# Moving table work, one transpose and two halves of a product in a hand-ordered four-engine pipeline (state-space convolution and routed low-rank FFN in fp32)

## The reference, cut to what matters

```python
# cond: a long convolution for each of 64 heads h, 64 states n
dtA = A * dt[:, None]                                   # A = -exp(log_A_real) + i A_imag
Cs  = Cc * (exp(dtA) - 1.0) / A
K   = 2.0 * einsum('hn,hnl->hl', Cs, exp(dtA * l)).real  # l = 0..1023
y   = irfft(rfft(u_m) * rfft(K)) + u_m * D               # u_m: u cut at each row's length
y   = y * mask
# ffn: 64 experts of rank 16, the top 16 of them for each token
scores = y @ Wr.T
gates  = softmax(top16(scores))                          # G: 0 for the other experts
h      = einsum('nd,krd->nkr', y, A)
out    = x + 2.0 * einsum('nkr,kdr->nd', h * G, B)
```

## Time and profile before

| | |
|---|---|
| median of 3 executions | 911.78 us |
| profiled execution, its own time | 912.11 us |
| its span, first to last instruction | 910.3 us |
| TensorE busy | 888.9 us (98%), 4536 matmuls |
| VectorE busy | 738.4 us (81%) |
| ScalarE busy | 380.7 us (42%) |
| 16 DMA engines | 40% of the span, 110 GB/s |
| mean granted TensorE clock | 0.998 |

### The profile page before, as it was taken

How to read it: one execution, slowest core, us unless ns; L and a number is a source line. 1 busy time by engine, 2 the same in 40 slices (tenths; PEclk the granted TensorE clock), 3 DMA queues, 4 the chain that set the end, 5 groups by cost and what they waited for, 6 DMA issues and landing times.

```text
span 910.3 us, 15546 instructions
## 1 busy us (share of the span) xinstructions
PE 888.9 (98%) x4536; PEld 791.5 (87%) x4536; DVE 738.4 (81%) x2473; ACT 380.7 (42%) x655; POOL 2.0 (0%) x12
## 2 busy tenths in 40 slices
PE   5999989999999999999999999999999999999998
PEld 4577978988999988899998899998889999889997
DVE  8899798888888888898888888888889888888722
ACT  4663344445334444434444533354443444442100
POOL 0000000000000000000000000000000000000000
PEclk9999999999999999999999999999999999999999
DMA  6631314443434443334443343444333444434331
GB/s 220 247 58 46 76 21 119 133 109 106 118 105 104 119 132 105 101 107 109 109 133 109 104 119 101 106 122 131 104 103 106 109 109 133 109 104 118 80 92 47
DMA packets 67123, 99.85 MB, mean 110 GB/s; under 512 B 22944, under 2 KB 49184, under 8 KB 67104
## 3 DMA queue, kind: packets, MB, share of 16 engines
q1 hardware_dynamic: 66400, 99.16, 39.8%
q10 hardware_dynamic: 704, 0.46, 0.2%
HBM read 60.52 MB, written 34.87 MB: 105 GB/s over the span
## 4 chain that ended last, share of the span: by engine, by line
PE 92%; DVE 4%; DMA 2%; ACT 1%; issue 1%; ACTq 0%; SPq 0%; DVEq 0%
PE out_ps L1239 25%; PE h_ps L1239 18%; PE out_ps L1243 12%; PE h_ps L1243 9%; PE turn_ps L1239 8%; PE turn_ps L1243 4%; PE conv_ps L1195 1%; PE conv_ps L1196 1%; PE conv_ps L1197 1%; PE h_ps L1248 1%; PE conv_ps L1178 1%; PE conv_ps L1179 1%; DMA b_in<-in_b_t 1%; PE conv_ps L1180 1%; PE conv_ps L1205 1%; PE conv_ps L1206 1%
## 5 line engine op out<-in xcount | busy, mean ns | idle before, releaser
L1239 PE MATMUL out_ps<-b_lo,g_hi 128*128 128x512 f32 x496 | 195.5, 394 | 0.0
L1239 PE MATMUL out_ps<-b_hi,g_hi 128*128 128x512 f32 x496 | 195.0, 393 | 0.0
L1239 PE MATMUL h_ps<-a_hi,y_hi 128*128 128x384 f32 x480 | 161.4, 336 | 0.0
L1239 PE MATMUL h_ps<-a_lo,y_hi 128*128 128x384 f32 x480 | 161.3, 336 | 0.0
L1243 PE MATMUL out_ps<-b_hi,g_lo 128*128 128x512 f32 x496 | 123.0, 390 | 0.0
L1243 PEld LDWEIGHTS out_ps<-b_hi,g_lo 128*128 128x128 f32 x496 | 93.1, 188 | 20.4
L1239 PEld LDWEIGHTS out_ps<-b_lo,g_hi 128*128 128x128 f32 x496 | 93.2, 188 | 19.6
L1239 PEld LDWEIGHTS out_ps<-b_hi,g_hi 128*128 128x128 f32 x496 | 93.2, 188 | 18.8
L715 DVE SCALAR_TENSOR_TENSOR z<-swapped,step_other,part 128x64 f32<-128x64 f32 x384 | 92.3, 281 | 12.0
L708 DVE SCALAR_TENSOR_TENSOR part<-z,step_own,conv_ps 128x64 f32<-128x64 f32 x384 | 90.3, 277 | 8.5
L1243 PE MATMUL h_ps<-a_hi,y_lo 128*128 128x384 f32 x480 | 93.1, 336 | 0.0
(11 more groups left out here) (216 smaller groups left out, 1496.6 us busy)
## 6 DMA issues: line engine op xcount, KB each, us to landing
xt_in<-in_xt SPq DMA_DIRECT2D x32, 512.0 KB, 3.3
x_in<-in_x SPq DMA_DIRECT2D x62, 256.0 KB, 3.6
out<-x_in SPq DMA_DIRECT2D x62, 256.0 KB, 3.1
moved<-square_sb SPq DMA_DIRECT2D x28, 512.0 KB, 2.6
square_sb<-moved SPq DMA_DIRECT2D x112, 128.0 KB, 2.9
b_in<-in_b_t SPq DMA_DIRECT2D x8, 512.0 KB, 6.0
a_in<-in_a_t SPq DMA_DIRECT2D x8, 512.0 KB, 7.1
t_lo<-k_sb SPq DMA_DIRECT2D x62, 64.0 KB, 4.1
```

What stands on the lines that cost most here:

```text
L1239: pe.matmul(o, hi[:, c, :], moving[:, c, columns], start=first and c == order[0] and moving is w_hi, stop=False)
```

## The change

Five edits, all in the order of instructions or in a wait; no arithmetic is added or removed.

1. **First step, ScalarE.** The split of the last `b` piece, MIDST[5], moves from ahead of `whole_in(1)` and `exps(0)` to behind them.
2. **Third step.** `arguments(4)` moves ahead of the last three chunks of `states(3)` on VectorE, `sines(4)` and `decays(4)` ahead of `high_z(3)` on ScalarE, `make_powers(4)` ahead of the two `low_gated(2)`, `out_factors(4)` between them; `high_in(4)`, `low_in(4)` and `arguments(5)` come earlier. On TensorE `turn_in(4)` moves ahead of `down(2, 0)`.
3. **step(3), VectorE.** `make_powers(5)` moves from behind the gate parts to a place ahead of the last three chunks of `states(4)`.
4. **step(3), TensorE.** `down(2, 1)` moves ahead of `kernel_row(5)` (it stood behind it).
5. **Last tile.** In `last_down` the single wait for both `add_rows(30)` becomes one for each bank of `out_ps`.

In the code of `step`, t is 3 where `second` is true. The iteration variable of the loop and the code of all later iterations are the same.

```diff
--- before.py
+++ after.py
@@ -469,7 +469,7 @@
             sines(1)
             decays(1)
             theta(2)
-            for i in MIDST[2:]:
+            for i in MIDST[2:5]:
                 split_weights(i)
 
             def exps(t):
@@ -501,6 +501,8 @@
             def first_step():
                 whole_in(1, in_ps_1)
                 exps(0)
+                for i in MIDST[5:]:
+                    split_weights(i)
                 copy_k(1, k_ps_1)
                 for i in LATE[:2]:
                     split_weights(i)
@@ -536,17 +538,17 @@
             def third_step():
                 exps(2)
                 high_near(3)
+                sines(4)
+                decays(4)
                 high_z(3)
                 for n in range(2):
                     high_turned(2, n, 4, g_hi)
-                sines(4)
-                decays(4)
+                high_out(4)
+                high_in(4)
                 theta(5)
-                high_out(4)
                 for i in range(HT):
                     high_y(3, i)
                 high_x(4)
-                high_in(4)
                 copy_k(4)
                 tables(5)
 
@@ -1034,6 +1036,7 @@
                 first_states(3)
                 states(3, range(1, MIDDLE))
                 gate(2)
+                arguments(4)
                 states(3, range(MIDDLE, FED))
                 gates_of(2)
                 gate_part(2, 0)
@@ -1042,19 +1045,18 @@
                 low_z(3)
                 sum_gates()
                 gate_part(2, 2)
-                arguments(4)
+                make_powers(4)
                 low_gated(2, 0)
+                out_factors(4)
                 low_gated(2, 1)
-                make_powers(4)
-                out_factors(4)
                 for i in range(HT):
                     mask_y(3, i)
                 low_out(4)
+                low_in(4)
+                arguments(5)
                 for i in range(HT):
                     low_y(3, i)
                 low_x(4)
-                low_in(4)
-                arguments(5)
                 scale_of(2)
                 add_rows(2, 0)
                 add_skip(4)
@@ -1066,6 +1068,8 @@
                     first_states(t + 1)
                     states(t + 1, range(1, MIDDLE))
                 gate(t)
+                if second:
+                    make_powers(t + 2)
                 if conv:
                     states(t + 1, range(MIDDLE, FED))
                 gates_of(t)
@@ -1081,8 +1085,6 @@
                 if not second:
                     low_squares(t - 1)
                 if prep:
-                    if second:
-                        make_powers(t + 2)
                     out_factors(t + 2)
                 if conv:
                     for i in range(HT):
@@ -1359,8 +1361,8 @@
                 pe.wait_ge(s_hg, 9)
                 turn_hg((3, 2, 1, 0)).then_inc(s_turn, 1)
                 from_states(3)
+                turn_in(4)
                 down(2, 0)
-                turn_in(4)
                 kernel_row(4)
                 feed(4)
 
@@ -1381,19 +1383,23 @@
                     pe.wait_ge(s_hg, 3 * t + 3)
                     if second:
                         turn_in(t + 2)
+                        down(t - 1, 1)
                     kernel_row(t + 2)
                 if not conv:
                     for n, blocks in enumerate(((7, 6, 5, 4), (3, 2, 1, 0))):
                         pe.wait_ge(s_hg, 3 * t + 2 + n)
                         turn_hg(blocks).then_inc(s_turn, 1)
-                down(t - 1, 1)
+                if not second:
+                    down(t - 1, 1)
                 if prep:
                     feed(t + 2)
 
             def last_down(t):
                 pe.wait_ge(s_glo, 2 * t + 2)
-                pe.wait_ge(s_o, 2 * t)
                 for n, (o, columns) in enumerate(ENDS):
+                    if n < 2:
+
+                        pe.wait_ge(s_o, 2 * (t - 1) + n + 1)
                     product_high(o, y_hi, b_hi, b_lo, columns, range(NE), first=True)
                     product_low(o, y_lo, b_hi, columns, range(NE)).then_inc(s_down, 1)
```

## The result

The changed kernel takes 907.44 us (median of five executions, 907.34 to 908.63); the kernel before, five executions (the three given above among them), 912.92 us (911.59 to 913.27). The ratio is 0.995, 95% interval 0.9938 to 0.9961: faster by 0.4 to 0.6%. 907.6 us had been predicted. The profiled execution is one of the slower of its kernel: 908.42 us, span 906.6 us (before: 912.11 and 910.3).

A forecast was written before the change was run, and what follows sets the result against it. TensorE, busy 888.9 of 910.3 us, was taken as the bound, with only its idle time to win. Terms -1.3 - 3.4 + 1.65 - 1.2 = -4.2 us took 911.8 to 907.6 us, range 905.3 to 909.4.

The forecast's parts named there:

- gates of tile 0 earlier: First step: without the last b split ahead, `gates` comes 1.3 us earlier, counted as -1.3 us.
- `make_powers(4)` (less 1.3): Iteration 3, VectorE: it starts at 106.5 instead of 111.87, before taking off 1.3 us for the first step.
- feed(4) (less 1.3): Iteration 3, TensorE: starts at 114.9 instead of 118.08, -3.2 us, with a wait of 0.4 to 0.5 us left.
- `copy_k(5)` (less 1.3): ScalarE: follows kernel_row(5) behind down(2, 1), at 136.8 instead of 139.00, only 2.2 us earlier.
- near(5) (less 1.3): TensorE: starts at 153.6 instead of 157.01, after an idle wait of 3.8 us instead of 1.0.
- kept of iterations 3 and 4: Of 6.2 us gained on TensorE only 3.4 us remain at near(5), bound by VectorE's and ScalarE's chain.
- the clock behind near(5): After the 3.8 us wait TensorE's clock falls to 1.2 GHz, costing 1.65 us; bounds 0 and 3.4.
- last tile: TensorE's last tile: the wait of 0.92 us goes and its first matmuls take 0.27 us less, -1.2 us.
- no fall: Rival: the clock does not fall behind the 3.8 us wait ahead of near(5), giving 905.9 us; chance 0.30.
- rival (C): ScalarE: each table switch costs 1.4 us more in its new place, by the skill's rule, giving 908.9 us; chance 0.06.
- (D): ScalarE and VectorE chain hardly moves, near(5) gains only the first step's share: 910.9 us, or 909.3 without clock drop; chance 0.10.
- (E): Slower: half clock lasts through near(5), from_states(5) and down(3, 0), losing 8.2 us, giving 914.1 us; chance 0.03.

The follow-up runs named there:

- e3: Kernel before with only the later split of the last b piece and the per-bank waits of the last tile: 910.31 us, ratio 0.9974.
- e1: Changed kernel with kernel_row(5) ahead of down(2, 1) again, everything else kept: 904.93 us.
- e4: Changed kernel with 16 more matmuls (3.7 us), whose result nobody reads, behind feed(5): 906.12 us.
- e5: Changed kernel with arguments(6) right behind make_powers(5), and sines(6) and decays(6) ahead of high_z(4): 903.09 us, ratio to the kernel before 0.9901.
- e2: Changed kernel with the third step put back to the order of the kernel before: 912.55 us, ratio to the kernel before 1.0003.
- e7: Changed kernel with make_powers(5) behind the gate parts again: 907.69 us.
- e8: Changed kernel with 8 more matmuls (1.85 us) behind feed(5): median 906.09 us, three executions at 906.00 to 906.09, two at 907.46 and 907.60.
- e6: Kernel of e5 with add_skip(5) moved behind make_powers(6) and turn_powers(6): 902.99 us.

## Why the prediction was right

**Time**: 907.6 predicted, 907.44 measured, inside 905.3 to 909.4. The gain itself was forecast as 4.2 us. Measured it is 5.5 us by the two medians of five (912.92 us before, where the three executions known to the forecast gave 911.78), and 911.95 (see e3) - 907.41 = 4.5 us between executions with the same mean clock of 0.998. So the agreement to 0.2 us owes something to chance. The mechanism doesn't: the parts are where the forecast has them (clock times are the forecast's less 1.3 us for part 1), and between the two profiled executions they add up, 1.4 + 3.5 + 1.2 - 2.3 = 3.8 us against 910.3 - 906.6 = 3.7.

| step | predicted | measured |
|---|---|---|
| gates of tile 0 earlier | 1.3 us | 40.67 to 39.27: 1.4 us |
| ScalarE's spare time ahead of `z_hi(3)` | 0.3 us | 0.27 us |
| `make_powers(4)` (less 1.3) | 105.2 | 105.09 |
| feed(4) (less 1.3) | 113.6, wait 0.4 to 0.5 us | 113.28, wait 0.22 us |
| `copy_k(5)` (less 1.3) | 135.5 | 135.20 |
| `make_powers(6)` (less 1.3) | 139.9 | 139.68 |
| near(5) (less 1.3) | 152.3, wait 3.8 us | 152.12, wait 3.89 us |
| kept of iterations 3 and 4 | 3.4 us | 157.01 - 152.12 - 1.4 = 3.5 us |
| the clock behind near(5) | +1.65 us | +1.3 us between the medians, +2.3 us in the profiled execution |
| last tile | 1.2 us | 0.92 + 0.24 us |

What made it hold was to carry the gain past the two stalls that the change removes, to the next place where engines meet. TensorE alone gained 6 us up to up(4); near(5) needs `t_lo`, which stands in VectorE's queue, and that queue had been held by `decay(6)`, behind `copy_k(5)`. e1 shows this link (near(5) 1.0 us earlier when `copy_k(5)` is no longer late), e4 shows that TensorE has no part in it (3.7 us more work, near(5) at the same time), and e5 that nothing else holds it (without the table work there, no wait at all).

**The clock** was the least certain step, 0.48 against 0.30 for no fall. By the mean clock it fell in all five executions of the changed kernel (0.998 or 0.996, as against 0.999 or 1.000 in e1, e4 and e5); where it fell is seen in the profiled one only. The price was sized from the one fall in the trace of before, 1.7 us. The profiled execution paid more, because the clock was down for 5.6 us of TensorE's work instead of 3.4: the mean clock differs like this between two executions of one kernel, and with it go the two kinds of times, 907.4 and 908.5. The step was a little too dear: 1.3 us by e4. Part of the reason is that the sum took matmuls at half clock to last twice as long. In the profiled execution those of near(5) follow each other at 0.43 us (152.70, 153.13, 153.56), in e4 at the upper clock at 0.23 us (152.47, 152.69, 152.93): 1.87 times. For 5.6 us this makes 2.6 us (an estimate), against 2.8 by the clock alone and 2.3 measured; the rest is open.

The two citations of the Trainium skill: the drain of 1.38 us at each table switch that "ScalarE: Activation LUTs" (section What ACT_TABLE_LOAD costs) adds was in no run; the sine starts 0.01 us behind its load and the decays 0.02 us behind theirs (99.35 and 101.31), and rival (C) is out. That a long wait puts TensorE back to half rate, as "TensorE: Matmul & The Clock Gate" has it, agrees with the windows above.

**Where the working was off.** Feed(4)'s wait was 0.22 and not 0.4 to 0.5 us: `make_powers(4)` started 0.1 us earlier than forecast, and from there to feed(4) it took 8.2 us (113.28 - 105.09) and not 8.4. Half of these 0.2 us lies right behind `make_powers(4)`: the next instruction on VectorE came 0.61 us after it, where `out_factors(4)`, which reads its result, had come 0.73 us after it (112.60 - 111.87). And the prediction treats part 4 as an even exchange. It has in its own numbers that `copy_k(5)` gains only 2.2 us, since it now follows 5.5 us of matmuls, and that near(5) hangs on it, but not the conclusion: leaving out part 4 is 2.5 us faster (e1). Rivals (D) and (E) are excluded by near(5)'s place and by the recovered clock at 157.7.

The gain by parts, from the runs: parts 1 and 5 together 2.5 us (e3; their shares, 1.4 and 1.2 us, are read from the rows, neither ran alone); part 2 is worth 5.1 us within the whole (e2); part 3 nothing (e7); part 4 minus 2.5 us (e1). These are worth what they are beside the others: as steps, by medians, the way goes from 912.2 us (before) to 910.3 (parts 1 and 5, e3), 904.9 (parts 2 and 3 added, e1) and 907.4 (part 4 added).

## What to carry to other kernels

Follow a gain to the next point where two queues meet, and see there which queue is last; work that fills one engine's wait is free only if nobody waits for what it puts off (here `copy_k`). When a wait on TensorE can't be removed, two short ones far apart are better than one long one: e1's 1.41 and 1.03 us, 19 us apart, cost nothing beyond themselves, the single 3.89 us cost 1.3 to 2.3 us more at the lower clock. Close together they did not help: 1.09 and 2.37 us within 4 us went with a fall in the profiles of before, e2 and e3. And an order that helped one iteration is worth trying on its neighbour: the same move for tile 6 (e5) gave another 4.3 us.

## What the runs showed of the hardware that I had not expected

- Useless matmuls made the kernel faster: 3.7 us of them, in a wait, kept TensorE at 2.4 GHz and saved 1.3 us (e4, 906.12 against 907.44 us).
- With a wait of 2.07 us the lower clock came in two of five executions, by their mean clock, and not in the profiled one (e8); single waits of 1.0 to 1.5 us were followed by it in none that was profiled. So e8 has two times, 1.5 us apart.
- Of the transfers that ScalarE's splits wait for, any may be the late one: in one execution of e6 two middle pieces of `b` held it up for 0.76 and 1.88 us, in the kernel before the last one for 1.49 us, in e4 the last but one for 1.18 us, and in the others the last but one for 0.2 to 0.4 us or none.
